# A Mamba and FP8 feed-forward layer on one core: the first stage reordered, with two scans drawn into it

## What is computed

```python
# branch 1: Mamba, DI = 1024 channels, N = 16 states, R = 128
proj = einsum('blh,eh->bel', xn, Win)             # hs half and gate half
hs   = silu(causal_depthwise_conv(proj[:, :DI], 4 taps) + bconv)
ssm  = einsum('bdl,pd->blp', hs, Wx)              # dt_in (R), B (N), C (N)
dt   = softplus(dt_in @ Wdt.T + bdt)
h_t  = exp(A * dt_t) * h_{t-1} + dt_t * B_t * hs_t    # per channel and state
y    = sum_n C_n * h_n + hs * D
out1 = (y * silu(gate)) @ Wout.T
# branch 2: xn, weights and activations cast to FP8 (e4m3)
out2 = (gelu(xn @ w0) * (xn @ w1)) @ w_linear
```

## Time and profile before

| | |
|---|---|
| median of 3 runs | 1075.25 us |
| profiled execution | 1076.49 us, its span 1074.7 us |
| busy, share of the span | DVE 95%, TensorE 85%, GpSimd 83%, ScalarE 77% |
| granted TensorE clock, mean | 0.957 of full |
| first stage, by DVE's first scan | 221.95 us |
| DMA | 150.24 MB, mean 140 GB/s; over 300 GB/s around 200 us |

### The profile page before, as it was taken

One profiled execution on the slowest core, in us unless ns is written; L12 is line 12 of the kernel. 1 busy time (PEld: TensorE's weight loads), 2 busy tenths in 40 slices (PEclk: granted clock), 3 DMA queues, 4 the chain that ended last, 5 costly groups with the idle time before them and its releaser, 6 DMA issues.

```text
span 1074.7 us, 14666 instructions
## 1 busy us (share of the span) xinstructions
PE 914.1 (85%) x4328; PEld 562.3 (52%) x4328; DVE 1016.8 (95%) x1214; ACT 828.2 (77%) x1154; POOL 891.5 (83%) x496
## 2 busy tenths in 40 slices
PE   3988888867877997898879979987998799879998
PEld 2756565534444564554445545555555455445554
DVE  7979898699999999999999999999999999999996
ACT  2777877678888865798887658988866689888662
POOL 4444445699999899989998999899989989998993
PEclk9999999979889999899999988999899899999999
DMA  7687768993111218532212183421212922212101
GB/s 282 192 261 245 272 225 316 363 365 133 54 60 40 88 41 274 185 122 74 80 39 88 40 302 140 137 79 59 75 54 70 341 97 101 79 59 79 40 0 40
DMA packets 53157, 150.24 MB, mean 140 GB/s; under 512 B 5728, under 2 KB 14048, under 8 KB 50016
## 3 DMA queue, kind: packets, MB, share of 16 engines
q1 hardware_dynamic: 53088, 149.41, 40.1%
HBM read 111.37 MB, written 38.01 MB: 139 GB/s over the span
## 4 chain that ended last, share of the span: by engine, by line
DVE 42%; issue 28%; PE 13%; ACT 10%; POOL 5%; DVEq 1%; DMA 1%; POOLq 0%; SPq 0%
DVE da L1100 18%; DVE prod L1075 11%; DVE hp L1100 8%; ACT da L994 3%; POOL dt_du L371 3%; PE mm L1135 2%; PE yT L1226 2%; DVE y L1083 2%; ACT L983 2%; ACT L982 2%; POOL hs_lo L366 2%; DVE gate_bf L1113 1%; PE proj L599 1%; PE proj L600 1%; PE proj L601 1%
## 5 line engine op out<-in xcount | busy, mean ns | idle before, releaser
L994 ACT ACTIVATE da<-unit,neg_a 128x512 f32<-128x512 f32 x512 | 338.6, 684 | 157.1 <-DVE prod L1075 154.0
L833 POOL TENSOR_TENSOR dbu<-unit,b_head 128x1024 f32<-128x1024 f32 x192 | 449.4, 2365 | 0.0
L1100 DVE TENSOR_TENSOR_SCAN da<-da,dbu 128x512 f32<-128x512 f32 x352 | 416.7, 1213 | 1.2
L1226 PE MATMUL yT<-ident,prod 128*128 128x128 f32 x1408 | 227.3, 290 | 94.7 <-DVE prod L1075 94.0
L1226 PEld LDWEIGHTS yT<-ident,prod 128*128 128x128 f32 x1408 | 167.8, 147 | 229.4 <-DVE prod L1075 189.9
L1063 POOL TENSOR_TENSOR hp<-hp,c_head 128x512 f32<-128x512 f32 x128 | 163.3, 1276 | 50.7 <-DVE gate_bf L1116 46.2
L1100 DVE TENSOR_TENSOR_SCAN hp<-da,dbu 128x512 f32<-128x512 f32 x160 | 192.6, 1204 | 3.3 <-ACT da L994 3.3
L1075 DVE TENSOR_TENSOR prod<-da,c_head 128x512 f32<-128x512 f32 x256 | 170.2, 665 | 0.0
L1175 PE MATMUL mm<-xn_b,w_sb 128*128 128x512 fp8e4 x512 | 141.9, 409 | 16.5 <-ACT acc L1014 12.9
L833 POOL TENSOR_TENSOR dbu<-unit,b_all 128x1024 f32<-128x1024 f32 x64 | 151.3, 2364 | 0.0
L1187 PE MATMUL mm<-xnT_b,wgate 128*128 128x512 f32 x256 | 128.7, 600 | 0.0
(11 more groups left out here) (118 smaller groups left out, 1285.5 us busy)
## 6 DMA issues: line engine op xcount, KB each, us to landing
unit<-unit_d SPq DMA_DIRECT2D x32, 768.0 KB, 4.4
unit_d<-dt_du SPq DMA_DIRECT2D x32, 512.0 KB, 2.7
wf<-in_wffn SPq DMA_DIRECT2D x12, 1024.0 KB, 6.5
c_head<-bc_d SPq DMA_DIRECT2D x24, 512.0 KB, 4.1
b_head<-bc_d SPq DMA_DIRECT2D x18, 512.0 KB, 4.8
unit_d<-hs SPq DMA_DIRECT2D x32, 256.0 KB, 6.7
w_sb<-w_d SPq DMA_DIRECT2D x64, 128.0 KB, 4.0
wgate<-in_win_gate SPq DMA_DIRECT2D x32, 256.0 KB, 2.8
```

The costliest lines, as they stand in the source:

```text
L833: return nc.gpsimd.tensor_tensor(dbu[:, n % DBUS:n % DBUS + NS, :], twice, b_all[n // NS], ALU.mult)
L994: nc.scalar.activation(da[n % SLOTS][:, :], unit[:, k % 2, 0, :], ACT.Exp, scale=neg_a[:, k, n:n + 1]).then_inc(da_ready, 1)
L1100: nc.vector.tensor_tensor_scan(state, da[n % SLOTS][:, :], dbu[:, n % DBUS, :], 0.0, ALU.mult, ALU.add).then_inc(scanned, 1)
L1226: ins = nc.tensor.matmul(yT[k % 2][:, t * P:(t + 1) * P], product[:, t * P:(t + 1) * P], ident[:, :], start=False, stop=last, is_transpose ...
```

## The change

In the first stage:
- **Tables ahead.** A_log is loaded right after the first x; its exp and negation come before the transposes' copies on ScalarE and before the low parts of x on DVE, where they were behind tap(0) and conv(0). The silu table is asked for at the start of each batch and after the deviation. In the last batch the exp table is asked for before the sums, not behind them.
- **Low parts of x on GpSimd** for the next batch, all four behind hs_lo(7); for the first batch they stay on DVE. TensorE does the transposes 2 and 3 together ahead of the last sums, ScalarE copies all tiles ahead of dtin.
- **Chunks.** DVE casts after conv(2), conv(5) and conv(7); SP handles a chunk before hs(2), before hs(5) and behind hs(7). The load of the first chunk of a batch is issued behind the stores of dt_du of the batch before.
- **B and C by batches.** b_head goes behind the stores of dt_du, and behind it c_head, four states a batch in three batches (1 MB each). The last batch loads no part of c_head. One semaphore, c_head_loaded, stands for them.
- **Two scans early.** In the last batch ScalarE makes the decays of states 0 and 1 of the first unit and then the skip term before dtin; DVE does the scans of both and the product of state 0 before bc; GpSimd makes the first pair of dbu behind hs_lo(5). The second stage begins its first unit at state 2.

The core of the diff:

```diff
@@ sync_a
             load_x(0)
+            sp.dma_start(neg_a[:, :, :], alog).then_inc(alog_loaded, 16)
...
-                    if not (last and i == CHUNKS_PER_B - 1):
+                    if i < CHUNKS_PER_B - 1:
                         load_chunk(c + 1)
...
                 for k in range(KU):
-                    if k % 3 == 0:
+                    if k in (2, 5):
                         chunk(k // 3)
...
-                    if last and k >= 2:
-                        g = k - 2
-                        sp.dma_start(c_head[:, g * NS:(g + 1) * NS, :]...).then_inc(c_loaded[g], 16)
-                    elif last:
+                    if last and k < 2:
                         u = k
                         sp.dma_start(unit[:, u, :, :]..., row(unit_d, u)).then_inc(unit_loaded[u], 16)
+                chunk(CHUNKS_PER_B - 1)
                 wait(bc_copied, b + 1)
                 sp.dma_start(row(bc_d, b), bc[:, :]).then_inc(bc_stored, 16)
+                for k in range(KU):
+                    wait(du_ready, b * KU + k + 1 + KU)
+                    sp.dma_start(row(unit_d, b * KU + k)[:, 0:2 * L], dt_du[:, k % DTS, :, :]...)
                 if not last:
+                    load_chunk((b + 1) * CHUNKS_PER_B)
                     wait(bc_stored, 32)
                     first, states = b * (G_PER_B * NS), G_PER_B * NS
                     sp.dma_start(b_head[:, bass.ds(first, states), :]...).then_inc(b_head_loaded, 16)
-                for k in range(KU):
-                    wait(du_ready, b * KU + k + 1 + KU)
-                    sp.dma_start(row(unit_d, b * KU + k)[:, 0:2 * L], dt_du[:, k % DTS, :, :]...)
+                    wait(xn_ready, b + 2)
+                    sp.dma_start(c_head[:, bass.ds(first, states), :]...).then_inc(c_head_loaded, 16)
@@ gpsimd_a
                     nc.gpsimd.tensor_tensor(hs_lo[:, k % 2, :], hs[:, k, :], hs_hi[:, k % 2, :], ALU.subtract)
+                    if last and k == KU - 3:
+                        head_start(pool, 0)
                 if last:
-                    head_start(pool)
+                    for n in range(NS, EARLY, NS):
+                        head_start(pool, n)
+                if not last:
+                    for h in range(HT):
+                        pool.wait_ge(xnT_ready, (b + 1) * HT + h + 1 + 2)
+                        nc.gpsimd.tensor_tensor(xnT_lo[:, h, :], xnT[:, h, :], xnT_hi[:, h, :], ALU.subtract).then_inc(lo_ready, 1)
@@ vector_a
-                    if k in (1, 4, 7):
+                    if k in (2, 5, 7):
...
-                if not last:
-                    low_tiles(b + 1, 0, HT - 1)
...
+                if last:
+                    first_scans(dve)
                 dve.wait_ge(bc_low_copied, b + 1)
...
-                if not last:
-                    low_tiles(b + 1, HT - 1, HT)
@@ scalar_a
+                nc.scalar.preload_act_table_set("silu_and_others")
                 for k in range(1, KU):
...
                     if k == 3 and not last:
                         deviation(b + 1)
+                        nc.scalar.preload_act_table_set("silu_and_others")
...
                 if not last:
-                    copy_tiles(b + 1, 1, HT - 1)
+                    copy_tiles(b + 1, 1, HT)
                 if last:
-                    skip_unit(act, 0, 0)
+                    first_decays(act)
...
-                nc.scalar.preload_act_table_set("natural_log_exp_and_others")
                 if not last:
-                    copy_tiles(b + 1, HT - 1, HT)
+                    nc.scalar.preload_act_table_set("natural_log_exp_and_others")
@@ tensor_a
                 if not last:
-                    transposes(b + 1, 2, 3)
+                    transposes(b + 1, 2, HT)
                 ssm_inputs(KU - 1)
-                if not last:
-                    transposes(b + 1, 3, 4)
@@ stage_b, new (SOON = 2)
+        def first_decays(act):
+            act.sem_inc(prod_used, PROD.total)
+            act.sem_inc(hp_used, HP.total)
+            nc.scalar.preload_act_table_set("natural_log_exp_and_others")
+            act.wait_ge(unit_loaded[0], unit_loads(0, 0))
+            act.wait_ge(handed.proj_ready, B * KU)
+            for n in range(SOON):
+                decay(act, 0, n)
+            skip_term(act, 0, 0)
+        def first_scans(dve):
+            dve.wait_ge(handed.proj_ready, B * KU)
+            for n in range(SOON):
+                scan(dve, 0, 0, n)
+                if n > 0 and n - 1 in OWN[0]:
+                    times_c(dve, 0, 0, n - 1, True)
```

More of the change, by code:

```diff
@@ L125, in build @@
         b_head_loaded = both.enter_context(nc.semaphore("b_head_loaded"))
+        c_head_loaded = both.enter_context(nc.semaphore("c_head_loaded"))
         c_loaded = [both.enter_context(nc.semaphore(f"c_loaded{g}")) for g in range(G)]
         unit_loaded = [both.enter_context(nc.semaphore(f"unit_loaded{i}")) for i in range(2)]
-        ahead = b_head, c_head, unit, b_head_loaded, c_loaded, unit_loaded
+        ahead = b_head, c_head, unit, b_head_loaded, c_head_loaded, c_loaded, unit_loaded
         def sem(name):
@@ L150, in _ @@
         def _(dve):
-            first.vector(dve)
+            first.vector(dve, second.first_scans)
             second.vector(dve)
@@ L155, in _ @@
         def _(act):
-            first.scalar(act, second.skip_term)
+            first.scalar(act, second.first_decays)
             second.scalar(act)
@@ L167, in stage_a @@
     xnT_d, xn8_d, unit_d, bc_d, w8_d = dram
-    b_head, c_head, unit, b_head_loaded, c_loaded, unit_loaded = ahead
+    b_head, c_head, unit, b_head_loaded, c_head_loaded, c_loaded, unit_loaded = ahead
     with ExitStack() as ctx:
@@ L422, in vector_a @@
                 if k == WINS:
+                    dve.wait_ge(neg_a_ready, 1)
+                    nc.vector.tensor_scalar(neg_a[:, :, :], neg_a[:, :, :], -1.0, None, ALU.mult).then_inc(neg_a_ready, 1)
                     low_tiles(0, 0, HT)
@@ new lines, in c_landed, with times_c @@
+        def c_landed(eng, b, n, opening):
+            if n >= G_AHEAD * NS:
+                eng.wait_ge(c_loaded[n // NS], b * 16 + 16)
+            elif opening:
+                eng.wait_ge(c_head_loaded, 16 * (B - 1))
+            else:
+                eng.wait_ge(c_loaded[n // NS], b * 16)
+        def times_c(dve, b, k, n, opening):
+            slot = PROD.slot(k, n)
+            dve.wait_ge(scanned, (b * KU + k) * N + n + 1)
+            dve.wait_ge(prod_used, PROD.slot_left(b, k, n))
+            if k == 0 and (n % NS == 0 or n - 1 not in OWN[k]):
+                c_landed(dve, b, n, opening)
+            nc.vector.tensor_tensor(prod[:, slot, :], da[n % SLOTS][:, :], c_all[n // NS][:, n % NS, :], ALU.mult).then_inc(prod_ready, 1)
@@ new lines, in scan @@
+        def scan(dve, b, k, n):
+            u = b * KU + k
+            dve.wait_ge(da_ready, u * N + n + 1)
+            dve.wait_ge(dbu_ready, u * N + n + 1)
+            state = da[n % SLOTS][:, :]
+            if n in POOLED[k]:
+                dve.wait_ge(hp_used, HP.slot_left(b, k, n))
+                state = hp[:, HP.slot(k, n), :]
+            nc.vector.tensor_tensor_scan(state, da[n % SLOTS][:, :], dbu[:, n % DBUS, :], 0.0,
+                                         ALU.mult, ALU.add).then_inc(scanned, 1)
@@ L966, in body @@
                 first = opening and k == 0
-                for n in range(N):
+                for n in range(SOON if first else 0, N):
                     if n == GELU and 1 <= k <= FFN_UNITS:
@@ L1092, in body @@
                 first = opening and k == 0
-                for n in range(N):
-                    dve.wait_ge(da_ready, u * N + n + 1)
-                    dve.wait_ge(dbu_ready, u * N + n + 1)
-                    state = da[n % SLOTS][:, :]
-                    if n in POOLED[k]:
-                        dve.wait_ge(hp_used, HP.slot_left(b, k, n))
-                        state = hp[:, HP.slot(k, n), :]
-                    nc.vector.tensor_tensor_scan(state, da[n % SLOTS][:, :], dbu[:, n % DBUS, :], 0.0,
-                                                 ALU.mult, ALU.add).then_inc(scanned, 1)
+                for n in range(SOON if first else 0, N):
+                    scan(dve, b, k, n)
                     if n > 0 and n - 1 in OWN[k]:
-                        times_c(b, k, n - 1)
+                        times_c(dve, b, k, n - 1, opening)
                     elif n == 0 and k > 0:
-                        times_c(b, k - 1, N - 1)
+                        times_c(dve, b, k - 1, N - 1, opening)
                     elif n == 0 and not opening:
-                        times_c(b - 1, KU - 1, N - 1)
+                        times_c(dve, b - 1, KU - 1, N - 1, False)
                     if 1 <= k <= FFN_UNITS and n == GELU_USED:
```

58 lines of the change are left out of this document (23 added, 35 removed).

## The result

| | before | changed |
|---|---|---|
| median, runs side by side | 1076.32 us (1075.24 to 1078.3, 6 runs) | 1088.99 us (1085.46 to 1091.88, 6 runs) |
| profiled execution, its span | 1076.49, 1074.7 us | 1085.60, 1083.8 us |
| second stage begins on DVE | 221.95 us, state 0 | 231.56 us, state 2 |

The changed kernel is slower: ratio 1.0113, 95% interval 1.0097 to 1.0129. The forecast had the sign and the place, but only half of the size between the two profiles (+4.35 for +9.1 us of span) and a third of it between the medians (+12.7); the time lies above its range.

The account below looks back on a forecast made before the run. DVE bounds the second stage; before it no engine is full and instruction order decides. The terms sum to +4.35 us: 1080.8 us for the profiled execution, 1079.6 for the median, range 1070.5 to 1083.5.

Parts of the forecast that it names:

- opening, at the first T: Up to the first batch's T: table load and exp of A_log moved earlier, -0.2 us (-1.0 to +0.4).
- first tail, b_head and low parts: First batch, T to next C: b_head behind the dt_du stores -3.1 us, low parts of x on GpSimd -0.3.
- low parts, two other tails: Second and third batch, T to next C: low parts of x on GpSimd, -0.3 us a tail.
- second batch, C to T: Second batch: late first w chunk stalls DVE at its cast, partly in place of existing waits, +1.6 us.
- C to T: C is the start of a batch's second convolution, conv(1); T is the end of its conv(7).
- third batch, C to T: Third batch: late first w chunk stalls DVE, +1.85 us (0.6 to 3.4); second chunk's landing covered.
- last batch, C to T: Last batch: second w chunk lands behind 8.13 MB of queued transfers, at C + 23.5 to 24, +7.4 us.
- second stage: Second stage starts on DVE with state 2 after two early scans, -2.3 us (-2.8 to 0).
- A: Rival: w chunks land in 6.5 us and overtake the broadcasts in the queue; 1069.5 us, faster; chance 0.20.
- B: Rival: last batch's chunks land at C + 8.5 and near C + 19, +2.9 us there; 1073.7 to 1076.5; chance 0.22.
- C: Rival: GpSimd's subtractions and DVE's casts and normalise block each other, +1.3 us in three tails; 1083.5 us; chance 0.09.
- Rival D: Early scans don't pay: GpSimd or FFN products give back 2.3 us in the first two units; 1081.9; chance 0.07.

Follow-up runs that it names:

- experiment 1: Changed kernel, but each batch's first w chunk is loaded at once behind the last cast of the batch before: 1080.81 us, ratio 1.0036.
- experiment 4: Changed kernel without the two early scans, their decays and the product of state 0: 1089.91 us, ratio 1.0132.
- experiment 3: Changed kernel with chunks loaded at once, casts behind conv(1), conv(4), conv(7) and c_head parts in the last batch, all as before: 1071.80 us, ratio 0.9952.
- experiment 6: experiment 3 with the low parts of x back on DVE and the old order of copies and transposes: 1074.11 us, ratio 0.9974.
- experiment 5: experiment 3 without the early scans: 1073.39 us, ratio 0.9976.
- experiment 12: experiment 9 without the early scans: 1070.98 us, ratio 0.9947.
- experiment 8: experiment 3 with SP confirming the first stage's stores ahead of the loads of the second w_gate and w_ffn tiles: 1071.55 us, ratio 0.9955.
- experiment 7: experiment 1 with c_head parts loaded in the last batch as before; casts stay behind conv(2), conv(5), conv(7): 1079.01 us, ratio 1.0024.
- experiment 2: Changed kernel with c_head loads of one state a batch instead of four: 1083.19 us, ratio 1.0052.
- experiment 10: Changed kernel with casts and c_head loads as in experiment 3; only each batch's first chunk is still loaded late: 1088.46 us, ratio 1.0109.
- experiment 9: experiment 3 with b_head issued behind the fourth store of dt_du, not the eighth: 1069.99 us, ratio 0.9945.
- experiment 11: experiment 3 with b_head ahead of the stores of dt_du again, as in the kernel before: 1073.89 us, ratio 0.9980.

## Why the prediction was right or wrong

The prediction's steps against the changed kernel's profile, us:

| step | predicted | measured |
|---|---|---|
| opening, at the first T | -0.2 | 0.0 (56.0 and 56.0) |
| first tail, b_head and low parts | -3.4 | -3.1 (23.43 for 26.56) |
| low parts, two other tails | -0.6 | +0.2 |
| second batch, C to T | +1.6 | +1.15 |
| third batch, C to T | +1.85 | +3.6 (28.57 for 24.95) |
| last batch, C to T | +7.4 | +8.4 (30.17 for 21.75) |
| last tail | 0 | -0.6 |
| second stage | -2.3 | -0.5 |
| sum | +4.35 | +9.1 |

*The mechanism was right in its main part.* The late chunk issued at C + 2.2, the second chunk of the last batch behind everything else at C + 24.5 (predicted C + 23.5 to 24), no wait for the dt_du stores, the hole in TensorE before the last sums (8.88 us): all are in the trace. Rivals A and B are false: T - C of the last batch lies above the forecast's. So is C: the fourth low part is ready at T + 8.6 (108.51 + 5.95 in the second tail), before its T + 8.8. Its sum was wrong besides: three tails at +1.3 in place of -0.3 are 4.8 us and not 3.9, which makes 1084.4; and A put +0.7 for stalls of 0.5 and 0.5. Two signs against the forecast came up: scans late at the start of the second stage (on decays, not on dbu), and wf landings of 7 us or less, in most loads (median 6.1), though not in the second chunks of batches two to four.

*The first step that failed: how the waits divide between the first and the second chunk.* I let the first chunk land near C + 9.5, by a landing of 8.2 us. Issued ahead of b_head, c_head and xnT_d, it came sooner: its cast starts at C + 8.4, C + 8.5 and C + 8.0 in batches two to four, after waits of 0.65, 0.78 and 3.47 us, where I had 1.6, 1.85 and 5. The second chunk came later than I had it. In the third batch I called it "covered": landing at C + 20.0, at 388 GB/s from C + 1.7, with conv(5) done at C + 21. In the changed kernel's profile it was cast at 151.97, C + 22.5, and conv(5) was done at 149.82, C + 20.3; the engines moved 348 GB/s there:

```profile
131.00:152.00 21.00, 18.72 (x73) 13.85 (x72) 17.39 (x34) 13.70 (x19) 7.13 (x6) 0.92 0.93 348
```

So the third batch's +3.6 for +1.85 is 0.78 before the first cast, 2.15 before the second and 0.7 for the new places of the casts by themselves: experiment 1 has C to T 25.7 there with no wait before these casts, for 24.95. I had priced the places at nothing; 0.4 of it is the cast behind conv(5), which took 1.62 us and not 1.22 since it met GpSimd. In experiment 4 the same load costs 0.68 us and not 2.15, so this wait is 0.7 to 2.2 us by the execution, and I had priced a margin of 1 us at 0. In the second batch the waits were 0.65 and 0.58 where I had 1.6 and 0: that its sum came out near (+1.15 for +1.6) is luck. The Trainium skill's figure ("DMA: Bandwidth & Descriptors", Specifications: about 358 GB/s from HBM for a core) fits the mean of this stretch better than mine, and the last batch worse (388 measured from 186 to 206 us). It was no ceiling in either: within this stretch the engines moved 412 GB/s from 136 to 140 us and 417 from 144 to 148.

*The second: a gain of 0.3 us left a tail after GpSimd's meeting with the cast.* I had taken 0.6 for the meeting out of a gain of 0.9 (the row of the last batch, 1.99 us, showed 0.7). Four subtractions take 5.93 us in the first tail of the changed kernel and 5.95 in the second, against 4.97 without a cast beside them (experiment 3): a block of 0.95 us in each tail. It takes back the whole gain of the move, which experiment 6 prices at 0.8 us a tail by the ratios and 1.3 by the profiles: the two tails without the change of b_head came out at +0.2 for -0.6. The Trainium skill's rule ("SBUF — State Buffer", SBUF: two separate sides: the port is an exclusive lock) agrees with these rows, which stand at the end; the sum that I gave by it was nearer.

*The third: the early scans at -2.3.* The second stage begins with state 2 when it would have begun with state 0, as I had it; but of the 2.83 us of work taken out of it about 1.0 stays gained (by its length in three pairs of profiles 0.8, 1.2 and 0.9; by the ratios 2.0, 2.6 and 0.2 us, each known to about 2). The rest is in three waits of DVE for decays, 1.8 us, where the kernel before waits for nothing up to 254 us:

```profile
243.92 2.35 DVE L888 TENSOR_TENSOR_SCAN da<-da,dbu 128x512 f32<-128x512 f32 x2 [0.37 <-ACT da L848]
...
247.63 1.22 DVE L888 TENSOR_TENSOR_SCAN hp<-da,dbu 128x512 f32<-128x512 f32 x1 [0.79 <-ACT da L848]
...
251.20 1.23 DVE L888 TENSOR_TENSOR_SCAN da<-da,dbu 128x512 f32<-128x512 f32 x1 [0.62 <-ACT da L848]
```

That the second stage is only 0.5 us shorter than before, and not 1.0, is another matter: without the early scans it took 852.9 to 853.1 us (experiments 4, 5 and 12), some 0.3 more than in the kernel before, which is not explained. Rival D is right in its mechanism: ScalarE's gelu waits for SP or, without that, for the FFN products whose weights come no sooner (experiment 8), and the decays behind it are late. I had looked for this only on GpSimd.

*The last batch* was 1.0 us short: its waits before the first and the second cast were 3.47 and 6.88 us for 5 and 5. By the order of the experiments its +8.4 are 0.8 for b_head (22.55), 3.45 for the casts' place (26.0), 1.8 for C (27.8) and 2.35 for the late chunk (30.2). My sum in bytes had them all in one. Its reason was not complete, though: I ascribed it to the late issue of the first chunk, and experiment 7 shows that the casts' place alone, with that chunk early, costs 3.45 us of it.

*What stays open.* The six times of the changed kernel spread over 6.4 us, those of experiment 4 over 6.8, those of experiments 2 and 10, which also have the late chunk, over 4.7 and 4.3, those of experiments 1, 3, 5 to 9 and 12 over 0.2 to 3.1. But those of experiment 11, without a late chunk, spread over 5.4. The profiled execution is one of the two fastest of the changed kernel. So 3.6 us, between the step in the two profiles (+9.1) and in the medians (+12.7), lie in executions of which there is no trace. That the late chunks land at other times in each would fit, and the 1.9 us between the third batches of the changed kernel and of experiment 4 speak for it; it is not shown for the whole.

## What to carry to other kernels

With one buffer, moving the instruction that empties it moves the next load too, past everything that the queue holds by then: price a moved cast by when its successor's load is issued, and count the bytes ahead of it. Where that sum ends within a few us of the moment at which the data are wanted, half a stall belongs in the forecast, not none. Work drawn forward over a stage's border is worth what the slowest of the other engines' first inputs allow; here one us of 2.8.

## What was not expected of the hardware

Where DVE's w cast (1.22 us alone) and a subtraction of GpSimd (1.28 us alone) meet, the one that comes second waits for the end of the other. The changed kernel shows both cases in its second tail:

```profile
107.27 1.28 POOL L367 TENSOR_TENSOR hs_lo<-hs,hs_hi 128x512 fp32r<-128x512 f32 x1 [0.96 <-ACT hs_hi L557]
...
108.11 1.52 DVE L474 TENSOR_SCALAR w<-wf 128x2048 fp8e4<-128x2048 f32 x1 [2.24 <-DMA wf<-in_wffn]
...
108.51 5.95 POOL L376 TENSOR_TENSOR xnT_lo<-xnT,xnT_hi 128x512 fp32r<-128x512 f32 x4
```

The cast comes into hs_lo(7), which ends at 108.55, and ends at 109.63, 1.08 us behind it; the first subtraction comes into the cast, and the four take 5.95 us and not 4.97. The same 1.08 to 1.09 us lie between the two ends at 151.97 (1.62 us; GpSimd's ends at 152.51) and at 198.11 in experiment 7 (1.95 us). The other way round, in the last batch of the kernel before, the cast was there first: it took its 1.23 us, and hs_lo took 1.99 and ended 1.11 us behind it. So a meeting costs the second, and the first nothing.

And TensorE's clock fell in the middle of the first stage, where DVE normalises and TensorE waits for it: from 144 to 148 us of the changed kernel TensorE was busy for 2.08 of 4 us, and in the next 4 us the granted clock was 0.60 (between its levels of 1.2 and 2.4 GHz), with 12 products in 4.00 busy us, where there were 20 from 136 to 140. A gap of this size need not do it: in experiment 3 TensorE was busy for 2.35 of 4 us from 94 to 98, and the granted clock stayed at 1.00 to 102. The rows of the changed kernel:

```profile
136.00:140.00 4.00, 4.00 (x20) 3.16 (x19) 3.00 (x9) 2.91 (x4) 0.71 (x1) 1.00 1.02 412
...
144.00:148.00 4.00, 2.08 (x9) 1.33 (x8) 3.93 (x7) 1.64 (x3) 0.17 (x1) 0.98 1.03 417
148.00:152.00 4.00, 4.00 (x12) 3.10 (x12) 1.78 (x4) 2.81 (x5) 2.06 (x2) 0.60 0.81 322
```
